# Three banks shared in turn by transposed scores, turned outputs and turned maxima, one bank for the product with V, and another order of the list of tiles

## The reference, cut to what matters

```python
x = L0_attn_content                      # 4 batches x 1024 tokens x 256
# attention on a layer norm of x: 16 heads of 16, softmax over ALL keys, then the causal mask
scores = einsum('bqhd,bkhd->bhqk', Q, K) / 4
alpha = where(causal, softmax(scores), 0)
x = x + layernorm(einsum('bhqk,bkhd->bqhd', alpha, V))
# mixture of 8 experts, the best 2 of each token, hidden size 1024
h = gelu(layernorm(x) @ w_fc[e]); out += combine[:, e] * (h @ w_proj[e])
x = x + layernorm(out)
```

## Time and profile before

| | us |
|---|---|
| median of 3 runs (1548.51 to 1550.6) | 1549.6 |
| the profiled execution, its own time | 1549.0 |
| its span, first to last instruction | 1547.1 |
| PE, DVE, ACT, POOL busy in it | 1420.5, 925.6, 805.0, 610.7 |

### The profile page before, as it was taken

How to read it: one execution, slowest core, us unless ns; L and a number is a source line. 1 busy time by engine, 2 the same in 40 slices (tenths; PEclk the granted TensorE clock), 3 DMA queues, 4 the chain that set the end, 5 groups by cost and what they waited for, 6 DMA issues and landing times.

```text
span 1547.1 us, 28642 instructions
## 1 busy us (share of the span) xinstructions
PE 1420.5 (92%) x9774; PEld 822.8 (53%) x9775; DVE 925.6 (60%) x1740; ACT 805.0 (52%) x1717; POOL 610.7 (39%) x729
## 2 busy tenths in 40 slices
PE   6788999999999999999999997989999999999990
PEld 3444233333333233323332333789999999999990
DVE  4587778777888988898888977761111111111115
ACT  5454777777777777777777787221111111111114
POOL 2234434443454445444444442323333333333335
PEclk9999999999999999999999999999999999999995
DMA  3665632112210222022204141656666666666646
GB/s 126 150 159 136 232 42 42 19 24 42 42 31 12 42 42 36 6 42 42 42 1 96 55 137 61 187 136 174 193 174 177 192 173 176 194 173 177 193 113 221
DMA packets 100405, 166.85 MB, mean 108 GB/s; under 512 B 12400, under 2 KB 67568, under 8 KB 100304
## 3 DMA queue, kind: packets, MB, share of 16 engines
q1 hardware_dynamic: 86192, 146.08, 35.2%
q0 software_dynamic: 13632, 18.69, 7.5%
q10 hardware_dynamic: 480, 0.79, 0.3%
HBM read 130.76 MB, written 34.77 MB: 107 GB/s over the span
## 4 chain that ended last, share of the span: by engine, by line
PE 69%; DVE 17%; issue 6%; ACT 5%; POOL 2%; DMA 2%; ACTq 0%; POOLq 0%; DVEq 0%
PE ps L1206 16%; PE ps L1220 16%; PE ps L1104 11%; DVE negmax L1701 10%; PE ps L1074 9%; PE ps L1261 8%; ACT wfc L921 2%; PE ps L1043 2%; PE ps L1067 2%; POOL wfc L833 1%; DVE x L1519 1%; PE ps L1248 1%; PE ps L1193 1%; DVE mv L1508 1%; ACT yx L848 1%
## 5 line engine op out<-in xcount | busy, mean ns | idle before, releaser
L1701 DVE TENSOR_REDUCE negmax<-ps 128x1 f32<-128x1024 f32 x512 | 606.8, 1216 | 133.9 <-PE ps L1261 132.4
L921 ACT ACTIVATE wfc<-ps 128x512 f32<-128x512 f32 x768 | 436.0, 595 | 166.2 <-PE ps L1074 160.4
L976 ACT ACTIVATE wfc<-ps 128x512 f32<-128x512 f32 x142 | 84.8, 597 | 426.3 <-PE ps L1206 399.6
L1206 PE MATMUL ps<-yx,wfc 128*128 128x128 f32 x2272 | 268.1, 276 | 5.3 <-issue 5.3
L1206 PEld LDWEIGHTS ps<-yx,wfc 128*128 128x128 f32 x2272 | 266.2, 193 | 9.5 <-issue 6.3
L1220 PE MATMUL ps<-arena,wfc 128*128 x1136 | 258.7, 381 | 0.3 <-issue 0.3
L765 POOL TENSOR_TENSOR wfc<-wfc,causal 128x512 f32<-128x512 f32 x128 | 162.5, 1270 | 243.2 <-issue 111.3
L821 POOL DMA_INDIRECT expert_out<-wfc,rt x71 | 112.7, 1587 | 299.6 <-DVE wfc L1665 289.2
L1220 PEld LDWEIGHTS ps<-arena,wfc 128*128 128x128 f32 x1136 | 211.4, 191 | 26.9 <-issue 0.8
L1261 PE MATMUL ps<-arena 96*128 96x512 bf16 x704 | 211.6, 382 | 8.6 <-DMA arena<-qk_parts 5.3
L1074 PE MATMUL ps<-arena 120*128 120x512 bf16 x528 | 202.3, 390 | 12.0 <-ACT wfc L921 0.4
(11 more groups left out here) (208 smaller groups left out, 1259.7 us busy)
## 6 DMA issues: line engine op xcount, KB each, us to landing
wfc<-in_L_ffn_w_fc SPq DMA_DIRECT2D x71, 1024.0 KB
arena<-qk_parts SPq DMA_DIRECT2D x126, 128.0 KB, 5.4
qk_parts<-x SPq DMA_DIRECT2D x32, 384.0 KB, 2.8
arena<-in_L_ffn_w_proj SPq DMA_DIRECT2D x8, 1024.0 KB, 8.6
wfc<-qk_parts SPq DMA_DIRECT2D x60, 128.0 KB, 5.5
expert_out<-rt SPq DMA_DIRECT2D x3, 1408.0 KB, 12.2
yx<-in_L_attn_content SPq DMA_DIRECT2D x8, 512.0 KB, 4.3
x<-in_L_attn_content SPq DMA_DIRECT2D x1, 4096.0 KB, 14.1
```

The source lines that it names most:

```text
L921: nc.scalar.activation(et_sb[b % NET][:, hl, :], bk(ebank(c, g)), ACT.Exp).then_inc(s_expB, 1)
L976: nc.scalar.activation(hidT[s][:, 4 * hf:4 * hf + 4, :], bk(1 + hf).rearrange("p (c t) -> p c t", c=4), ACT.Gelu).then_inc(s_ge, 1)
L1206: ins = nc.tensor.matmul(bk(1 + hf)[:, c * P:(c + 1) * P], w1[s][:, kc * FF + (4 * hf + c) * P:kc * FF + (4 * hf + c + 1) * P], xsT[:, kc, :],
L1701: nc.vector.tensor_reduce(negmax[:, hl % 2, i:i + 1], ps[:, 2 * (k % 2):2 * (k % 2) + 2, :], AX.XY, ALU.max, negate=True).then_inc(s_max, 1)
```

## The change

Chunks, turns and turned maxima now share the banks 4, 5 and 6, in the order in which PE issues them. The function `ring_entries` writes this order out, and entry n waits for whatever frees entry n-3: the exponential of a chunk (`s_expB`), ACT's copy of maxima (`s_mtc`), or DVE's norm of a turn (`s_norm`). A pass has 70 entries: 64 chunks, 2 turns and 4 maxima. The last group is no exception any more. The product with V uses bank 7 for both halves, so that the first burst of a half waits for the copy of the half before it. The norm stands in the unit of its turn (3 and 13, before 5 and 15).

Ahead of the experts: `list_early` is a unit later and ahead of `count`, the gathers of the first tiles are two units earlier, some steps of the layer norm and of `place` of the last four tiles are one or two units later, the first tile is transposed in bank 2, and in the late list the pieces and products of tiles 5 to 7 stand in another order, with `copy_x(5, 1)` ahead of the chain that makes the list.

```diff
-        at_norm = [x + 2 for x in at_turn]
+        at_norm = list(at_turn)
...
-        at_bn_x, at_var_x, at_root_x, at_scale = (4, 42), (5, 44), (5, 44), (7, 46)
+        at_bn_x, at_var_x, at_root_x, at_scale = (4, 44), (5, 45), (5, 45), (7, 46)
...
-        at_place = [x + 11 for x in at_first]
-        AT_TOTALS, AT_LIST, AT_TAKE, AT_INDEX, AT_ROWS, AT_TURN0, AT_COPY0, AT_FIRST = 25, 28, 29, 31, 36, 39, 40, (43, 44)
+        at_place = [x + 11 + 2 * (i == IN_TAIL - 1) for i, x in enumerate(at_first)]
+        AT_TOTALS, AT_LIST, AT_TAKE, AT_INDEX, AT_ROWS, AT_TURN0, AT_COPY0, AT_FIRST = 25, 29, 29, 31, 34, 39, 40, (43, 44)
...
+        def ring_entries():
+            out = []
+            for x in range(PRO, (NGR + 2) * U):
+                p, k = divmod(x, U)
+                out += [("turn", p - back, j) for j, back in due(at_turn, k) if live(p, back)]
+                chunks = [("chunk", p - back, c) for c, back in due(at_chunk, k) if live(p, back)]
+                out += chunks[:1]
+                out += [("maxima", p - back, hl) for hl, back in due(at_m, k) if live(p, back)]
+                out += chunks[1:]
+            return out
...
+            def ring_free(kind, g, x):
+                n = SLOT[kind, g, x] - NRING
+                if n < 0:
+                    return
+                last, g, x = RING[n]
+                if last == "chunk":
+                    pe.wait_ge(s_expB, NCH * g + x + 1)
+                elif last == "turn":
+                    pe.wait_ge(s_norm, 2 * g + x + 1)
+                else:
+                    pe.wait_ge(s_mtc, GH * g + x + 1)
...
-                    wait_pos(pe, s_expB, NCH * g + c - 1)
+                ring_free("chunk", g, c)
...
-                    et, out = et_sb[b % NET], bk(6 + hf)
+                    et, out = et_sb[b % NET], bk(7)
...
-                        wait_pos(pe, s_norm, 2 * (g - 1) + (j + 1))
-                        pe.wait_ge(s_mtc, min(GH * g + M_BEFORE_PV[j], NH) if isinstance(g, int) else
-                                   GH * g + M_BEFORE_PV[j])
+                        wait_pos(pe, s_poc, 2 * g + j)
...
                         pe.wait_ge(s_poc, 2 * (p - back) + (j + 1))
+                        ring_free("turn", p - back, j)
...
-            first_half(5, 1, 0)
+            first_product(5, 1)
             list_late(0)
-            first_half(5, 1, 1)
             list_late(1)
-            list_late(2)
```

More of the change, by code:

```diff
@@ L467, in x_bank, with tx_bank @@
             return 0 if i < IN_TAIL or kc == 0 else 4
+        def tx_bank(t):
+            return 2 if isinstance(t, int) and t == 0 else 7
         def at_tail(x, p, k):
@@ L515, in load_side, with ring_bank @@
                    .then_inc(s_ld[u], 16)
+        def ring_entries():
[8 more added lines that the diff above has]
+            return out
+        RING = ring_entries()
+        NRING = 3
+        SLOT = {x: n for n, x in enumerate(RING)}
+        R0 = (2 - SLOT["turn", NGR - 1, 1]) % NRING
+        def ring_bank(kind, g, x):
+            return 4 + (SLOT[kind, g, x] + R0) % NRING
         def turn_bank(hl, g):
-            return 7 if isinstance(g, int) and g == 0 else 6 + HALVES[M_HALF[hl]]
+            return 7 if g == 0 else ring_bank("maxima", g, hl)
+        assert PRO > U + max(at_m) - U and ring_bank("turn", NGR - 1, 1) == 6
         @block.sync
@@ L910, in body @@
                         g = p - back
+                        bank = bk(ring_bank("chunk", g, c))
                         act.wait_ge(s_ST, NCH * g + c + 1)
@@ L915, in body @@
                                 wait_pos(act, s_dt, g - 2)
-                            nc.scalar.activation(bk(ebank(c, g)), bk(ebank(c, g)), ACT.Exp,
+                            nc.scalar.activation(bank, bank, ACT.Exp,
                                                  accum_out=den_u[:, (u - back) % NSL, hl, i:i + 1]).then_inc(s_expB, 1)
@@ L920, in body @@
                         wait_pos(act, s_pv, NBU * g + b - NET + 1)
-                        nc.scalar.activation(et_sb[b % NET][:, hl, :], bk(ebank(c, g)), ACT.Exp).then_inc(s_expB, 1)
+                        nc.scalar.activation(et_sb[b % NET][:, hl, :], bank, ACT.Exp).then_inc(s_expB, 1)
             root_c(0, 0)
@@ L1060, in chunk @@
                 g, v = p - back, (u - back) % NSL
[L1061 to L1064 removed]
+                ring_free("chunk", g, c)
                 if is_corner(c):
                     hl, i = divmod(c // 4, HQ)
[L1067 removed]
+                    nc.tensor.matmul(bk(ring_bank("chunk", g, c)), qs[v][0:MROW + MR, hl, i * P:(i + 1) * P],
                                      ks[v][0:MROW + MR, hl, 512:1024], start=True, stop=True).then_inc(s_ST, 1)
@@ L1187, in transpose_x @@
             def transpose_x(t, s):
[L1188 to L1189 removed]
+                if isinstance(t, int) and t == 1:
+                    pe.wait_ge(s_poc, 2 * NGR)
                 pe.wait_ge(s_xs[s], 16 * (t // 2 + 1) if isinstance(t, int) else t * 8 + 8 * (2 - s))
@@ L1267, in body @@
                         h = GH * (p - back) + hl
-                        if isinstance(p, int) and h == GH:
-                            pe.wait_ge(s_poz, 1)
                         pe.wait_ge(s_sp, 4 * h + 4)
                         turned[0] += 1
-                        past = p - M_AFTER_NORM[hl]
-                        wait_pos(pe, s_norm, 2 * past + (M_HALF[hl] + 1) if not isinstance(p, int) or past >= 0 else 0)
+                        if p - back:
+                            ring_free("maxima", p - back, hl)
                         nc.tensor.matmul(bk(turn_bank(hl, p - back))[MROW:MROW + MR, 0:P],
@@ L1786, in _ @@
                 gates(i)
+            copy_x(5, 1)
             link(nc.vector.scalar_tensor_tensor(out=u_8, in0=k_128, scalar=-1.0 / P, in1=ntile[:, :],
@@ L1823, in _ @@
             copy_x(6, 0)
-            for q in range(4, NPR // PCE):
+            for q in range(4, 6):
                 hot(q)
             copy_y(5, 1)
+            for q in range(6, NPR // PCE):
+                hot(q)
+            copy_x(7, 1)
             nc.vector.tensor_reduce(tabf[:, 0:NLC], cmp_l[0:1, :, :], AX.X, ALU.add).then_inc(s_hic, 1)
```

49 lines of the change are left out of this document (17 added, 32 removed).

## The result

| | before | after |
|---|---|---|
| median, us | 1550.1 | 1611.7 (1610.5 to 1614.6) |
| ratio, 95% interval | | 1.0405 [1.0391, 1.0418] |
| span of the profiled execution, us | 1547.1 | 1610.5 |
| mean granted clock | 0.979 | 0.963 |

The change costs 61.6 us. The forecast was 1584.7, and 1611.7 is what the third rival gave (1607 to 1613).

What follows compares the result with a forecast made beforehand. PE's order of work was taken as the bound. Attention +43.5, behind the last pair +1.5, into the experts -2.5 and late list -7.4 summed to +35.1 on a median of 1549.6: 1584.7 us, range 1555 to 1613.

Steps and rivals of the forecast that it cites:

- the third rival: In the attention PE's clock falls behind the new waits, 1.6 to 2 us once a pass: 1607 to 1613 us, chance 0.16.
- The bound: In an attention pass PE's order of work bounds, not yet DVE; PE needs 44.8 of 50.2 us, about 5.4 are waits.
- The third bank: In units without a burst, chunks no longer wait for ACT's exponentials: -2.35 us a pass, up to 4.9.
- DVE's lag: In passes with layer norms DVE lags behind the faster PE at its extra steps: 1.3 us instead of today's 0.74.
- The second rival: ACT's own pace sets the units without a burst, so the extra bank removes no waits: 1618 us, chance 0.08.
- The copy in unit 2: With one bank for the product, PE's burst in unit 2 waits for DVE's copy of unit 1: +1.40 us a pass.
- unit 13, +0.1: The new burst stands behind the turn, which already waits for the other copy: about +0.1 us a pass.
- The norm in units 4 and 14: The first chunk of each unit waits for DVE's norm of the turn: +1.7 and +1.6 us, or +2.0 with layer norms.
- The sum of a pass: All attention terms together: +2.45 us without layer norms, +3.5 with; passes of 52.7 and 54.4 us.
- The first rival: In the attention PE's new pauses let DVE catch up, +0.5 us a pass: 1541 to 1550 us, chance 0.14.
- Behind the last pair and into the experts: Chunk waits for the late norm in pass 16, +1.5 us; last turn's copy goes ahead of `place`, -2.5 us.
- The late list: Up to the product of tile 7, the new order with `copy_x(5, 1)` earlier removes PE's waits: -7.4 us.

Runs made afterwards that it cites:

- run 7: The kernel before, with only DVE's copy and norm moved to the start of their units: 1543.6 us, ratio 0.9957.
- run 1: The changed kernel, with DVE's copy and norm both ahead of the maximum of their unit: 1515.0 us, ratio 0.9776 against the kernel before.
- run 6: As run 1, but with a ring of two banks instead of three: 1607.4 us, ratio 1.0364 against the kernel before.
- run 2: The changed kernel, with only DVE's norm ahead of the maximum of its unit: 1543.9 us, ratio 0.9958 against the kernel before.
- run 5: The kernel before, with only the new order of the late list on PE and DVE: 1542.3 us, ratio 0.9944.
- run 3: The changed kernel, with only DVE's copy ahead of the maximum of its unit: 1568.5 us, ratio 1.0122 against the kernel before.

## Why the prediction was right, and where not

**The bound.** PE's order of work with DVE close behind: right. With the new waits gone a pass is 47.75, where PE's own work was counted as 44.8 (its terms add up to 44.9).

**The third bank, -2.35 a pass.** Against run 7, which has DVE's order too, run 1 is 2.12 shorter without layer norms: the size is right. With them it is 1.09, where the bank and the 0.56 for DVE's lag make 1.8. The second rival (nothing removed) is out: 367 waits for exponentials became 119, and run 6 costs 92 us. What I read wrongly is what the bank is for, as run 6 showed.

**The copy in unit 2, +1.40, and unit 13, +0.1.** The runs give 1.8 to 2.2. The pause of the burst is 1.66. Before, the burst started 0.68 ahead of the copy (444.36, 445.04); now PE is ready for it 0.93 ahead (518.55, 519.48), so that it waits 0.26 longer for the same copy than forecast. That was omitted. Why the pass loses a further 0.1 to 0.5 is not shown.

**The norm in units 4 and 14, +3.3, or 3.7 with layer norms.** The runs give 2.7 to 3.2. The pauses are 1.73 (1.87 worked out) in unit 4, and in unit 14 1.93 without layer norms (2.07) and 2.32 with them (2.45).

**The sum of a pass**: 52.7 and 54.4 forecast, 52.69 and 54.35 measured in passes at full clock. The terms for the copy (too small) and for the norm (too large) err in opposite directions, and the terms with layer norms add up to +3.4, not to the +3.5 used; the agreement to 0.1 is luck in part. The first rival, that DVE's lag vanishes (50.7 and 51.5), did not happen.

**The clock.** This is the step that failed: the sum has no term for it, and it cost 22.9 of the 27.0 us by which the time is above 1584.7. I set rows 10 (1.97, clock 1.00) against it and gave the fall 0.16, though three pauses of 1.4 to 2.5 were to come in each of 14 passes. One row in which the clock held was no evidence for some forty more pauses. The trace of the kernel before had more on it. Of its four pauses of over 1.5 between 903 and 1041 us, the one of 1.97 alone has no fall beside it. That of 2.46 has the one of the earlier trace rows, and those of 3.11 (up to 945.84) and 4.18 (up to 1021.89) have these:

```profile
945.00:951.00 6.00, 4.81 (x63) 2.67 (x67) 4.70 (x40) 1.29 (x4) 0.00 (x0) 0.50 0.93 333
1020.00:1026.00 6.00, 4.11 (x22) 4.08 (x23) 2.13 (x6) 0.32 (x1) 2.58 (x2) 0.50 0.58 196
```

The rival's price per fall, 1.6 to 2, was right (1.6). That its count of one in each pass came close (15 in 14 passes) is luck: a pass had between none and three. Its reason, the nearness of the waits in units 13 and 14, doesn't hold either: ten of the fifteen falls lie elsewhere, and run 2 had falls behind a pause with none near it.

**Behind the last pair and into the experts, +1.5 and -2.5.** Together +3.5 instead of -1.0. In run 1 the same stretch is 80.48, 5.0 less than in after. Of after's pauses in it, the 1.37 of unit 2 and the 2.49 of unit 4 are under 1 us there, and that for `oh_bf` is 2.39 instead of 3.64, so the same waits behind the last pair are most of what costs here. I had counted them (+1 and +3.2) and then, it seems, taken off too much for the catching up; no run separates that part. The -1.5 of run 1 against before is too small to be told from none.

**The late list, -7.4.** -7.1 in after and -7.3 in run 5.

## What to carry to other kernels

When a buffer moves into a ring, the moment of its release counts: look where the releasing instruction stands in the in-order stream of its engine, and what it waits for there. Here a copy and a norm of 0.7 us each, written behind a maximum that waits for PE, cost 5 us a pass, and moving them ahead of it turned a loss of 4% into a gain of 2.2%. New pauses of PE that recur and are as long as those here (1.66 to 2.33 us) should be priced with the clock from the start, and repeated work that fills them is a quick test of that price.

## What the runs showed of the hardware

The same pause lets the clock fall in one pass and not in the next. In run 2 (norm first) the pause in unit 2 is 1.66 in every pass. PE's timeline in two passes, and the clock behind each:

```profile
293.77 0.41 PE L1122 MATMUL ps<-wfc,vone 128*17 128x128 f32 x8 [1.66 <-DVE wfc L1748]
...
344.43 0.41 PE L1122 MATMUL ps<-wfc,vone 128*17 128x128 f32 x8 [1.66 <-DVE wfc L1748]
...
295.00:296.00 1.00, 1.00 (x13) 0.28 (x3) 0.00 (x0) 0.00 (x0) 0.00 (x0) 0.50 0.00 0
...
345.00:346.00 1.00, 1.00 (x18) 0.43 (x11) 0.00 (x0) 0.00 (x0) 0.19 (x1) 1.00 0.00 0
```

In that kernel it fell behind unit 2 in two of 14 passes, in the changed kernel fifteen times. In run 3 it fell behind unit 14 in six, once behind 1.93 and then behind 2.33 in every other pass, though the pauses of all these passes are the same. Each fall in the passes lasts a little over 3 us at 0.50 and costs 1.6, whatever the pause before it was. The Trainium skill, "TensorE: Matmul & The Clock Gate", section "What's actually happening", says that the chip's look at PE's activity is free-running and is not reset when a kernel starts. The repeated pause with two outcomes agrees with that; that this is the cause was not tested by any run here. What stays open is the chance with which a pause of a given length leads to a fall. In the 14 passes pauses of 0.97, four in each pass of run 6, led to none, nor did those of 0.90 in the kernel before or of 0.53 in run 1; the shortest with a fall right behind it there is 1.66. But that is no safe length: behind the last score pair of run 6 the clock is at 0.50 from 972 to 975 us, and the longest of PE's pauses in the 8 us before is 0.97 (up to 966.04), with 0.54 and 0.47 behind it.
